# Products that nobody reads between the products of the last two node pairs in a two-layer graph network kernel

## The reference

```python
h = concat([x[src], x[dst], edge_features]) @ W1 + b1
h = relu(layernorm(h) * ln_g + ln_b)
messages = (h @ W2 + b2) * sigmoid(edge_features @ gate_w + gate_b)
agg = segment_sum(messages, dst, num_segments=n)
gi, gh = agg @ W_ih.T + b_ih, x @ W_hh.T + b_hh      # 3 x 128 columns each
r, z = sigmoid(i_r + h_r), sigmoid(i_z + h_z)
n = tanh(i_n + r * h_n)
out = (1 - z) * n + z * x
x = layernorm(x + out)
```

## Time and profile before

| | |
|---|---|
| time, median of 3 runs | 4724.15 us (4723.77 to 4759.89) |
| device time of the profiled execution | 4727.02 us |
| its span, first to last instruction | 4725.2 us |
| granted PE clock, mean over the span | 0.838 of full speed |
| PE, DVE, POOL busy | 71%, 76%, 67% |

### The profile page before, as it was taken

How to read it: one execution, slowest core, us unless ns; L and a number is a source line. 1 busy time by engine, 2 the same in 40 slices (tenths; PEclk the granted TensorE clock), 3 DMA queues, 4 the chain that set the end, 5 groups by cost and what they waited for, 6 DMA issues and landing times. The chain is left out here.

```text
span 4725.2 us, 106818 instructions
## 1 busy us (share of the span) xinstructions
PE 3372.5 (71%) x20905; PEld 2951.6 (62%) x20906; DVE 3588.0 (76%) x14556; ACT 2370.6 (50%) x6569; POOL 3177.1 (67%) x3367
## 2 busy tenths in 40 slices
PE   6642666666666666666664778888888888888887
PEld 4541556555555555555564667777777777777775
DVE  8995777777777777777776778777777777777775
ACT  2210323333443334433342666777777777777775
POOL 0003777777777777777774777777777777777773
PEclk9655777777777778777776999999999999999997
DMA  3102445555555555555553444444444444444442
GB/s 115 47 27 75 144 135 146 147 148 148 147 146 147 147 146 148 148 148 148 148 146 109 118 107 114 115 115 114 115 116 115 115 115 114 115 115 116 114 115 54
DMA packets 597448, 574.46 MB, mean 122 GB/s; under 512 B 320589, under 2 KB 462931, under 8 KB 597308
## 3 DMA queue, kind: packets, MB, share of 16 engines
q0 software_dynamic: 133632, 328.29, 25.9%
q1 hardware_dynamic: 463676, 244.70, 19.0%
HBM read 535.82 MB, written 43.09 MB: 123 GB/s over the span
## 5 line engine op out<-in xcount | busy, mean ns | idle before, releaser
L1788 POOL DMA_INDIRECT front_rows<-c,gather_index x1660 | 1574.2, 948 | 525.7 <-issue 505.4
L743 POOL DMA_INDIRECT front_rows<-bx,gather_index x832 | 790.3, 950 | 255.3 <-issue 249.8
L743 POOL DMA_INDIRECT bxrows<-bx,gather_index x828 | 782.9, 946 | 252.5 <-issue 250.9
L1822 PE MATMUL pre<-w1e,efT 128*128 128x129 f32 x3328 | 680.1, 287 | 160.0 <-DVE h L2042 150.8
L1470 DVE TENSOR_TENSOR acc<-acc,scattered 128x129 f32 x1664 | 468.3, 281 | 327.9 <-ACT mask L1377 319.4
L1294 PE MATMUL pre<-near,hotT 128*128 x3328 | 557.9, 337 | 218.9 <-DVE h L1447 175.9
L1294 PEld LDWEIGHTS pre<-near,hotT 128*128 128x128 f32 x3328 | 522.2, 246 | 266.9 <-issue 263.1
L1824 PE MATMUL pre<-near,hotT 128*128 x3328 | 665.0, 283 | 0.0
L1822 PEld LDWEIGHTS pre<-w1e,efT 128*128 128x128 f32 x3328 | 528.8, 200 | 186.5 <-DVE h L2042 157.1
L1473 DVE SCALAR_TENSOR_TENSOR hotw<-row_bank,places,mask 128x128 f32<-128x128 f32 x1664 | 574.0, 345 | 2.4 <-ACT mask L1377 2.2
L1370 ACT ACTIVATE sig<-logit,b 128x8 f32<-128x8 f32 x208 | 62.6, 301 | 972.5 <-DVE h L1454 971.9
(11 more groups left out here) (303 smaller groups left out, 6245.1 us busy)
## 6 DMA issues: line engine op xcount, KB each, us to landing
spread<-place_rows SPq DMA_DIRECT2D x416, 256.0 KB, 3.6
ef<-in_edge_attr SPq DMA_DIRECT2D x1664, 32.0 KB
front_rows<-c,gather_index POOLq DMA_INDIRECT x1660
front_rows<-bx,gather_index POOLq DMA_INDIRECT x832
bxrows<-bx,gather_index POOLq DMA_INDIRECT x828
x_turned<-x1T SPq DMA_DIRECT2D x98, 64.0 KB
g_xT<-x_turned SPq DMA_DIRECT2D x98, 64.0 KB
x_a<-in_x SPq DMA_DIRECT2D x97, 64.0 KB
```

Of the source, the lines that this page charges most:

```text
L743: nc.gpsimd.indirect_dma_start(out=there[:, k, 0:2 * D], out_offset=None, in_=s.bx[:, :], in_offset=bass.IndirectOffsetOnAxis(ap=s.index[: ...
L1788: pool.indirect_dma_start(out=crows[q][:, k, 0:D], out_offset=None, in_=s.c[:, :], in_offset=bass.IndirectOffsetOnAxis(ap=s.index[:, g * G ...
L1822: nc.tensor.matmul(pre[:, bank, at:at + W], efT[par][:, k // 2, :], w1e2[:, k % 2, :], start=True, stop=False)
```

## The change

A helper `stay_busy(i, times)` is added to PE's program in layer 2. For pairs 47 and 48 alone it waits for `pre_used` to be at its final value and then issues `times` products of the 128 x 128 identity with the 128 x 384 weight `wfold` into bank 0 of `pre`. Nothing reads them. It is called after each of a pair's three phases: once after T, three times after rz, twice after n. That is 12 products over the two pairs.

```diff
+                def stay_busy(i, times):
+                    if not isinstance(i, int) or i < PAIRS - 2:
+                        return
+                    pe.wait_ge(pre_used, 3 * GROUPS)
+                    for _ in range(times):
+                        nc.tensor.matmul(pre[:, 0, 0:3 * D], s.ident_f[:, :], wfold[:, :], start=True, stop=True)
+
                 def nodes(g, q, o):
                     i = pair_at(q, o, BEHIND)
...
                         last.then_inc(T_made, 1)
+                        stay_busy(i, 1)
                     i = pair_at(q, o, BEHIND + 1)
...
                         last.then_inc(rz_made, 1)
+                        stay_busy(i, 3)
                     i = pair_at(q, o, BEHIND + 2)
...
                         last.then_inc(n_made, 1)
+                        stay_busy(i, 2)
                 joined_slots(pe, steps, nodes, LAST)
```

## The result

| | before | after |
|---|---|---|
| median of 22 runs each | 4729.34 us | 4718.34 us |
| lowest | 4723.05 | 4715.91 |
| ratio, 95% interval | | 0.9957 (0.9938 to 0.9977) |
| device time of the profiled execution | 4727.02 | 4716.73 |
| its span | 4725.2 | 4714.9 |

The kernel became faster, by less than 1% as forecast, and its time of 4718.3 lies in the forecast range. But the kernel moved by more than the 7.8 us forecast: 11 us by the medians, some 20 by the ratio. In every set of several some executions take some 35 us longer, whatever the kernel (8 of these 22 before, 4 of 22 after, 4 to 8 of 12 later), and they weigh on ratio and median, so that from here on each "median" is of the other executions, and ratios are not used to tell kernels apart. By it the two kernels stand at 4728.1 and 4718.0, 10.1 apart. The profiled executions are 10.3 apart.

The account below looks back on a forecast made before the run. PE's stages at 1.2 GHz in a slackless chain of waits were taken to bound the last 40 us. Gains of 8.56 less 0.8 delay gave 7.8 us, so 4724.15 became 4716.4, range 4713 to 4725.

Parts of the forecast that it names:

- what bounds the end: Last 40 us: a chain of waits from PE to ACT or DVE and back, without slack; shorter PE stages show in full.
- The gains by stage: Pairs 47 and 48: PE stages at 2.4 GHz instead of 1.2 from 4688.7 on, together 8.56 us less.
- the wait costs nothing: Added wait for `pre_used` in layer 2: met 18 us ahead with nothing queued behind it, so 0.
- the releaser of rz: rz of pair 48: transposed x by DMA could come late and lose T's 0.5 us; taken as 0.
- the delay by the products: Products outlasting the gaps after T, rz and n: 0.8 us late in all, bounds 0 and 1.4.
- the row with the pause: An rz product of 256 columns after a pause, 0.64 us at 2.4 GHz; gave 0.86 as upper bound per added product.
- the close-following row: An rz product of 256 columns following closely, 0.43 us at 2.4 GHz; gave 0.65 as lower bound per added product.
- the clock stays high throughout: Pairs 47 and 48: clock at 1.00 from 4683.6 to the end of pair 48's n; chance 0.60.
- the first rival: Clock falls once more, at the end of pair 47's n: gain 4.3 us, 4718 to 4723; chance 0.22.
- up to 2.9 more: Runs where the old kernel's rz of pair 47 ran at 1.2 GHz: extra saving, setting the low end at 4713.
- nothing: Only long gaps cost the clock, so filling short ones changes nothing: 4724, give or take 1; chance 0.10.
- slower: Clock falls at 4690 as before and products stand in the way at 1.2 GHz: 4.7 us more, 4728.9; chance 0.08.

Follow-up runs that it names:

- none after n: The changed kernel without the two products after each n: tail 38.9 us, median 4719.2 us, where the old kernel beside it had 4727.1.

## Why the prediction was right or wrong

**Right: what bounds the end, and by how much the clock stretches it.** The hand-overs kept their lengths to 0.1 us, so that a change of a PE stage showed in full in the tail. The gains by stage were forecast as 2.57 (n of pair 47), 0.50 (T), 2.92 (rz) and 2.57 (n of pair 48), 8.56 together. Where the clock never fell, in the kernel helped from pair 46 on, they were 2.45, 0.47, 2.93 and 2.32 + 0.16 (n of pair 48 and the step to the end), 8.3.

**Right: the wait costs nothing**, by the kernel that has only the wait. The DMA did not become the releaser of rz either: T48 to rz48 is 1.44 to 1.45 with T at 2.4 GHz, as pair 47's 1.41.

**Mis-sized: the delay by the products, 0.8.** It was 0 at 2.4 GHz. The gaps are 2.07 and 1.6 and the products 0.63 to 0.71 each: rz to n is 5.51 with three of them and 5.52 without (the kernel before, pair 47); n to T is 4.93 with two and 4.92 without (none after n). I had taken 0.80, near the row with the pause, on the reason that each brings its own weights; the close-following row (0.43 x 1.5) was nearer. By luck this evened out a part of what the next point cost.

**Half right: the clock stays high throughout.** In two of three profiles it fell once, in the end of pair 47's n, which is the place the first rival named, and its price of 1.4 for the two products was measured as 1.34. The rest of that rival did not come: the two products brought the clock back before T of pair 48 had ended, so that T lost 0.1 and rz nothing. The prediction's reading ahead of it, that gaps in PE's work cost the clock, was too narrow: with products of two rows it fell without a gap. The changed kernel's tail was 34.5, 34.5 and 33.8, where the sum gave 41.4 - 7.8 = 33.6.

**Wrong: the base against which the sum was made.** The step that failed is "I set the sum against the median: 4724.15 - 7.8". The sum described one execution, in which rz of pair 47 had happened to run at 2.4 GHz. I treated it as the usual one, and took the other, at 1.2 GHz and "up to 2.9 more", for a low end only. The base was itself the upper of only two executions that count. In the 22 runs before, the median was 4728.1 and not 4724.15, 3.9 more; the profile at 4730.02 us shows an end that is 3.4 longer than that of the profile used. None of the three profiles of the changed kernel has that end: in the one where pair 47 began at 1.2 GHz, the clock was back with rz's first product, behind the product after T. What the change takes away is thus 6.9 or 7.6 us from the one end (41.4) and 10.3 or 11.0 from the other (44.8). Over all sets of several executions the medians are 4726.0 (63) and 4717.7 (22), 8.3 apart. Set by set the old kernel's were 4728.1, 4724.4, 4725.6 and 4727.1, the new one's 4718.0 and 4717.3, so the gain is 7.1 in one set and 10.1 in another, and it is the old kernel that moves. How much of that is its two ends, how much the stretch ahead, and how much the occasion (the three later ones were on three different chips) stays open. The time itself, 4716.4 forecast against 4718.0, was close by luck: the base was 3.9 too low and the gain 2.3 short of the 10.1 measured, and the two misses partly cancel.

Of the 10.3 us between the two profiles shown at the top, 6.9 are the change, by the tail; 2.2 are n of pair 46, whose clock varies in either kernel; and 1.2 lie ahead of it, which I did not follow up.

**The rivals "nothing" and "slower"** are out for these products, the second by what it named as its test: the clock after rz of pair 47 reads 1.00. With products of two rows the second is what happens.

**Against the rule of the Trainium skill.** It names long idle gaps between bursts as what brings the low clock back (TensorE: Matmul & The Clock Gate, Why this matters for your kernels). The traces do not agree that it takes one: the longest gap before the fall was 2.06 us in the kernel before, and in the kernel with two-row products the clock fell with PE busy 5.30 of 5.30 us.

## What to carry to other kernels

If a serial end of a kernel hands over between PE and other engines, look at the granted clock there. Where it reads 1.2 GHz, products of all 128 rows into a free bank, no longer together than each gap, can keep it at 2.4 GHz for nothing. Here the tail was 33.1 to 34.5 with every gap filled, 38.5 with twice the products, 38.9 with the place after n left out, and 43.5 with two of three places left out, each of the last three in one execution. Before making a sum against a profile, look whether the stage at hand ran at the same clock in other executions: a second profile of the old kernel showed the other end.

## What was not expected of the hardware

- Products of two rows did not hold the clock, though PE was shown busy 5.30 of 5.30 us before it fell and 9.00 of 9.00 while it stayed at 1.2 GHz. PE's busy share alone therefore did not tell whether the clock would hold. n, in which every second product has two rows, is where it fell in the changed kernel.
- Back to back, a float32 product of 384 columns took 0.63 us at 2.4 GHz (six in 3.80 us in the kernel with twice the products), although each brings its weights again.
